# A mixture-of-experts layer whose weighted result rows are sent to their token's place during the products

## The chip, the cores and the metric

The kernel runs on one core of one Trainium2 chip. The metric is the time of one execution on the device, in microseconds (us). A core has a matrix engine (TensorE, PE), a vector engine (VectorE, DVE), a scalar engine (ScalarE, ACT), GpSimd (POOL) and SyncE (SP). SP, ACT and POOL issue DMA transfers, which run on 16 DMA engines. All arithmetic here is float32 unless a row says otherwise.

## What is computed

The program is a decoder of two layers on `x` (4 batches of 512 tokens of 256 numbers). Everything but its last step is the same in both kernels. The last step is a mixture of 8 experts, of which each token uses 2:

```
def _L1_ffn_ref(x, Wg, bg, W1, b1, W2, b2):
    gate_scores = softmax(x @ Wg + bg)
    topk_scores, topk_idx = top_k(gate_scores, 2)
    topk_scores = topk_scores / (sum(topk_scores) + 1e-08)
    for e in range(8):
        h = gelu(x @ W1[e] + b1[e])
        y = h @ W2[e] + b2[e]
        output = output + y * combine_w[..., e:e + 1]
    return output
x = x + _L1_ffn_ref(_layernorm(x), ...)
```

`combine_w` holds a token's two normalised scores at its two experts. W1[e] is 256x1024 and W2[e] 1024x256, 1 MB each.

## The kernel before, in words

All of this is in `mixture`, the last function that runs. Token tile t (t = 0 to 15, four to a batch) holds 128 tokens, one per partition. There are 5 stages, each a block of one program per engine, ended by a barrier of all engines (line 69).

- **mi** (L2428 to L2463). SP loads the 2 MB of `xs` in one DMA (L2431), then the gate's small weights, and waits for all. DVE fills `hid` with zeros (L2439); ACT writes them over the whole of `x_by_expert` in DRAM in three DMAs (L2453). POOL and DVE make small constants.
- **mn** (L2466 to L2511). DVE takes mean and variance of all 16 tiles (`norm_stats`, L97 and L100), POOL raises the variances to the power of minus one half (L107), DVE normalises tile by tile into `xn` (L2481). PE transposes (L2496), ACT copies each batch to `xTall` (L2511). When all is transposed PE forms the gate's scores (L2502), and DVE adds the bias in 16 instructions (L2485).
- **mg** (L2514 to L2618). DVE picks two experts per token, counts, and works out for each of the 4096 (token, expert) pairs its row in a list sorted by expert in which each expert begins at a multiple of 256 rows (`pos`, L2580). POOL then sends the rows of `xn` there with 32 indirect DMAs of 128 rows of 1 KB (L2618, 16 tiles times 2 experts). Meanwhile PE and DVE add the experts' second biases to `xs` (L2609, L2583).
- **ex** (L2622 to L2732). The sorted list has NTL = 23 tiles of 256 rows. For each tile SP loads the expert's W1 and W2 (L2631, L2632, three slots) and the rows `xg` (L2635, three slots), PE transposes them (L2664), DVE copies the transposes to `xgT` (L2722), PE multiplies by W1 (L2676), ACT applies bias and gelu (L2711), PE multiplies by W2 (L2688), DVE copies each half of the result to `yg` (L2732), and SP stores it to `y_by_expert` (L2639). PE's order is: transpose and first product of tile t+1, then second product of tile t.
- **mo** (L2736 to end). POOL gathers the result rows of each token tile with 32 indirect DMAs (L2746) into eight buffers `got`, DVE multiplies each by the pair's weight and adds it to `xs` (L2756, 32 times), SP stores each finished tile in 16 DMAs (L2764).

SP's order in ex is written by hand: `wait turned, rows(t), wait down, weights(t), results(t - 3)`. The y of tile t, half a, is ready when `down` reaches 2t + a + 1.

Of the kernel before, what the change touches and what calls it, by code (L numbers as in the profile page):

```python
# [22 lines left out]
P = 128  # L23
# [2363 lines left out]
def mixture(nc, es, dram, x5, out, psum, ident, nhalf, b1c):  # L2387
# [5 lines left out]
    WS, XS, GS = 3, 3, 8  # L2393
    x_sorted = nc.dram_tensor("x_by_expert", [NTL * TL, C], F32, kind="Internal").ap()
    y_sorted = nc.dram_tensor("y_by_expert", [NTL * TL, C], F32, kind="Internal").ap()
    xs, xn = sb("xs", [P, NT, C]), sb("xn", [P, NT, C])
# [3 lines left out]
    xg, xgT = sb("xg", [P, XS, TL // P, C]), sb("xgT", [P, 2, KT, TL])  # L2400
    yg = sb("yg", [P, 2, TL // P, C])
    got = sb("got", [P, GS, C])
# [17 lines left out]
    eps_var, rstd = sb("mev", [P, NT]), sb("mrstd", [P, NT])  # L2420

    w_in = [es.enter_context(nc.semaphore(f"expert_weights_in{i}")) for i in range(WS)]
    x_in = [es.enter_context(nc.semaphore(f"expert_rows_in{i}")) for i in range(XS)]
    y_out = [es.enter_context(nc.semaphore(f"expert_rows_out{i}")) for i in range(2)]
    cleared = es.enter_context(nc.semaphore("sorted_cleared"))
    sent = es.enter_context(nc.semaphore("rows_sorted"))

    with stage(nc, "mi", "in_", "zeroed") as (block, in_, zeroed):  # L2428
        @block.sync
        def _(sp):  # L2430
            sp.dma_start(xs[:, :, :].rearrange("p (b t) c -> p b t c", b=B), x5.rearrange("b p t c -> p b t c")).then_inc(in_, 16)  # L2431
# [3 lines left out]
            sp.wait_ge(in_, 16 * 4)  # L2435

        @block.vector
        def _(dve):
            dve.memset(hid[:, :, :, :], 0.0).then_inc(zeroed, 1)  # L2439
            dve.memset(before_me[:, :], 1.0).then_inc(zeroed, 1)  # L2440
            dve.memset(all_ones[:, :], 1.0)
            dve.memset(restart[:, :, 1:NT], 1.0)
            dve.memset(restart[:, :, 0:1], 0.0)

        @block.scalar
        def _(act):
            act.wait_ge(zeroed, 1)
            zeros = hid[:, :, :, :].rearrange("p s f n -> p (s f n)")
            rows = x_sorted.rearrange("(p r) c -> p (r c)", p=P)
            at = 0  # L2450
            while at < NTL * TL * C // P:
                n = min(2 * FT * TL, NTL * TL * C // P - at)
                act.dma_start(rows[:, at:at + n], zeros[:, 0:n]).then_inc(cleared, 16)  # L2453
                at += n

        @block.gpsimd
        def _(pool):
            pool.iota(idx[:, 0, :], [[1, NE]], base=0, channel_multiplier=0)
            pool.iota(count_u[:, :], [[1, 24]], base=0, channel_multiplier=0)
            pool.wait_ge(zeroed, 2)  # L2460
            pool.affine_select(before_me[:, :], before_me[:, :], [[1, P]], ALU.is_gt, 0.0, base=0,
                               channel_multiplier=-1)
    n_cleared = 16 * -(-(NTL * TL * C // P) // (2 * FT * TL))  # L2463


    with stage(nc, "mn", "dc", "var_ready", "rstd_ready", "normed", "turned", "copied", "gated", "logged") as (  # L2466
            block, dc, var_ready, rstd_ready, normed, turned, copied, gated, logged):
        on_vector, on_pool = norm_stats(nc, "mn", xs, stats, mv, rstd, eps_var, nhalf, NT, (dc, var_ready, rstd_ready))

        @block.gpsimd  # L2470
        def _(pool):
            on_pool(pool)

        @block.vector
        def _(dve):
            then = chained(dve, dc)
            dve.tensor_copy(iota[:, :], idx[:, 0, :])
            dve.tensor_copy(counted[:, :], count_u[:, :])
            on_vector(dve, then)
            for t in range(NT):  # L2480
                dve.tensor_scalar(xn[:, t, :], xs[:, t, :], mv[:, t, 0:1], rstd[:, t:t + 1],  # L2481
                                  ALU.subtract, ALU.mult).then_inc(normed, 1)
            for t in range(NT):
                dve.wait_ge(gated, t + 1)
                dve.tensor_tensor(lg[:, t, :], psum[:, 6, t * NE:(t + 1) * NE], bg[:, :], ALU.add)  # L2485

        @block.tensor
        def _(pe):
            for b in range(B):
                if b >= 2:  # L2490
                    pe.wait_ge(copied, b - 1)
                for t in range(QT):
                    tt = b * QT + t
                    pe.wait_ge(normed, tt + 1)
                    for k in range(KT):
                        last = pe.transpose(psum[:, 2 * (b % 2) + k, t * P:(t + 1) * P],  # L2496
                                            xn[:, tt, k * P:(k + 1) * P], ident[:, :])
                last.then_inc(turned, 1)
            for tt in range(NT):
                pe.wait_ge(copied, tt // QT + 1)  # L2500
                for k in range(KT):
                    last = pe.matmul(psum[:, 6, tt * NE:(tt + 1) * NE], xTall[:, k, tt * P:(tt + 1) * P], wg[:, k, :],  # L2502
                                     start=(tt == 0 and k == 0), stop=(k == KT - 1), skip_group_check=True)
                if tt == NT - 1:
                    last.then_inc(gated, NT)

        @block.scalar
        def _(act):
            for b in range(B):
                act.wait_ge(turned, b + 1)  # L2510
                act.copy(xTall[:, :, b * T:(b + 1) * T], psum[:, 2 * (b % 2):2 * (b % 2) + 2, :]).then_inc(copied, 1)  # L2511

# [275 lines left out]
```

## Time and profile of the kernel before

| what | us |
|---|---|
| median of 3 runs (lowest, highest) | 4335.82 (4323.85, 4353.62) |
| the profiled execution, its own time | 4334.44 |
| its span, first to last recorded event | 4332.6 |

So 1.84 us lie around the span. Of the span PE was busy 80%, DVE 51%, ACT 38%, POOL 21%. Times in the rows below count from the start of the span. A row of the timeline has start, duration, engine, line and operation; in square brackets stands how long the engine was idle before it and what released it.

### The profile page before, as it was taken

To read this page: it belongs to the slowest core of one execution; us is meant where nothing else is said; L and a number is where in the kernel's file an instruction comes from. 1 tells how busy PE (TensorE), PEld (TensorE's weight loads), DVE (VectorE), ACT (ScalarE), POOL (GpSimd) and SP (SyncE) were. 2 spreads that over 40 slices of the span, in tenths; PEclk is the share of its full clock that TensorE was granted. 3 is DMA by queue.
4 is the path that set the end of the run, shared out by engine and by line. 5 is a ranking of instruction groups with operands and counts; after the bars stand their busy time and mean duration, and the time that the engine had idled before them with its cause. 6 is when DMAs were issued, how large, how long until landed. Compare 5 with 4: busy or idle time off the path is not lost. (4 is left out here: it accounts for less than half of the span.)

```text
span 4332.6 us, 56718 instructions
## 1 busy us (share of the span) xinstructions
PE 3450.6 (80%) x21582; PEld 1893.0 (44%) x21582; DVE 2230.4 (51%) x4281; ACT 1642.5 (38%) x2455; POOL 905.5 (21%) x989
## 2 busy tenths in 40 slices
PE   3887678898887588898887788988875788946995
PEld 2423453426324345245334535264244543435884
DVE  3465766553464855734557764634648656430002
ACT  1343653342343733333345642423437433401221
POOL 0110542101201722011104512012006320120002
PEclk9889789999899799999898798999998899958997
DMA  4111102201202011111102012011120011034553
GB/s 80 37 55 59 16 7 74 62 19 36 67 12 73 1 42 61 41 35 42 55 20 54 1 42 83 19 40 42 50 73 1 30 66 48 30 115 155 173 175 119
DMA packets 244259, 239.67 MB, mean 55 GB/s; under 512 B 111902, under 2 KB 209420, under 8 KB 241548
## 3 DMA queue, kind: packets, MB, share of 16 engines
q1 hardware_dynamic: 234224, 217.91, 16.7%
q10 hardware_dynamic: 6684, 9.63, 0.7%
q0 software_dynamic: 3072, 8.39, 0.6%
q8 instruction: 177, 2.90, 0.3%
q14 instruction: 102, 0.84, 0.1%
HBM read 167.20 MB, written 68.68 MB: 54 GB/s over the span
## 5 line engine op out<-in xcount | busy, mean ns | idle before, releaser
L857 ACT ACTIVATE prob<-psum 128x1024 f32<-128x1024 f32 x384 | 372.2, 1021 | 559.1 <-PE psum L777 559.1
L1184 ACT ACTIVATE prob<-psum 128x1024 f32<-128x1024 f32 (+3 forms) x384 | 331.6, 914 | 443.7 <-PE psum L1104 443.7
L898 DVE TENSOR_REDUCE scr<-psum 128x1 f32<-128x512 f32 x576 | 371.4, 685 | 216.7 <-PE psum L764 212.9
L1222 DVE TENSOR_REDUCE stats<-psum 128x1 f32<-128x512 f32 (+3 forms) x576 | 334.3, 620 | 165.7 <-PE psum L1092 161.0
L1104 PE MATMUL psum<-stack 32*128 32x512 f32 (+3 forms) x1536 | 213.3, 626 | 63.2 <-ACT prob L1184 33.1
L774 PE MATMUL psum<-stack 32*128 32x512 f32 x1536 | 228.6, 665 | 33.2 <-DVE xo L888 24.7
L395 PE MATMUL psum<-ident 128*128 128x128 f32 x1736 | 220.2, 287 | 14.6 <-PEq L1809 9.6
L395 PEld LDWEIGHTS psum<-ident 128*128 128x128 f32 x1736 | 214.3, 203 | 24.7 <-issue 23.9
L805 PE MATMUL psum<-prob,ones_f 128*32 128x512 f32 x1536 | 206.8, 606 | 0.0
L1119 PE MATMUL psum<-prob,vbig 128*32 128x512 f32 (+3 forms) x1536 | 194.4, 580 | 4.3 <-ACT prob L1184 4.3
L2676 PE MATMUL psum<-xgT,ew 128*128 128x256 f32 x736 | 167.0, 386 | 18.0 <-DVE xgT L2722 18.0
L2732 DVE COPY yg<-psum 128x256 f32<-128x256 f32 x46 | 19.5, 425 | 308.5 <-PE psum L2688 308.5
L2711 ACT ACTIVATE hid<-psum,b1c 128x256 f32<-128x256 f32 x184 | 77.1, 470 | 257.6 <-PE psum L2676 257.6
L894 DVE TENSOR_REDUCE scr<-psum 128x4 f32<-128x2048 f32 x48 | 108.8, 2289 | 123.7 <-PE psum L757 123.6
L1218 DVE TENSOR_REDUCE stats<-psum 128x4 f32<-128x2048 f32 (+3 forms) x48 | 97.2, 2025 | 135.8 <-PE psum L1081 135.8
L579 POOL TENSOR_TENSOR x<-x,rows 128x256 f32<-128x256 f32 x32 | 22.1, 723 | 671.9 <-ACTq L64 581.6
L2688 PE MATMUL psum<-ew,hid 128*128 128x256 f32 x736 | 162.4, 379 | 0.0
L1610 POOL TENSOR_TENSOR xo<-xa,rows 128x256 f32<-128x256 f32 x32 | 22.2, 725 | 661.3 <-POOLq L1359 661.3
L2676 PEld LDWEIGHTS psum<-xgT,ew 128*128 128x128 f32 x736 | 139.4, 192 | 42.1 <-DVE xgT L2722 23.7
L1092 PE MATMUL psum<-w_mlp,stack 96*128 96x512 bf16 x384 | 134.6, 411 | 26.2 <-DVE stats L1222 16.2
L764 PE MATMUL psum<-w_mlp,stack 96*128 96x512 bf16 x384 | 126.6, 399 | 30.5 <-DVE scr L898 29.8
L2688 PEld LDWEIGHTS psum<-ew,hid 128*128 128x128 f32 x736 | 139.8, 190 | 19.0
(444 smaller groups left out, 6690.6 us busy)
## 6 DMA issues: line engine op xcount, KB each, us to landing
ew<-in_L_ffn_W SPq DMA_DIRECT2D x46, 1024.0 KB, 7.5
stack<-q_terms SPq DMA_DIRECT2D x144, 128.0 KB, 2.4
w_mlp<-in_L_xattn_a_li_w SPq DMA_DIRECT2D x16, 1024.0 KB, 7.3
q_terms<-parts SPq DMA_DIRECT2D x96, 128.0 KB, 2.1
stack<-k_terms SPq DMA_DIRECT2D x72, 128.0 KB, 2.7
w_mlp<-k_terms SPq DMA_DIRECT2D x36, 256.0 KB, 4.4
w_mlp<-a_terms SPq DMA_DIRECT2D x36, 256.0 KB, 4.9
a_keys<-stack SPq DMA_DIRECT2D x4, 2048.0 KB, 6.3
```

The costliest lines, as they stand in the source:

```text
L395: pe.matmul(psum[:, bank, at:at + P], ident[:, :], ident[:, :], start=True, stop=True, skip_group_check=True)
L774: pe.matmul(psum[:, j, :], KTg[W * j:W * j + W, g, kt * P:(kt + 1) * P], QTg[W * j:W * j + W, g, :], start=True, stop=False)
L805: last = pe.matmul(psum[W * j:W * j + W, 7, :], ones_f[:, :], prob[:, (2 * n + j // 2) % 4, j % 2, :], start=(kt == order[0]), stop=(kt == ...
L857: act.activation(prob[:, i % 4, :, :], psum[:, 2 * p:2 * p + 2, :], ACT.Exp, scale=scale).then_inc(exped, 1)
L898: dve.tensor_reduce(found[:, c:c + 1], ring(i), AX.X, ALU.max).then_inc(freed, 1)
L1092: pe.matmul(ring(i)[:, 0:n], MQ[0:ROWS, g % 2, j, t * P:(t + 1) * P], MK[0:ROWS, g % 2, j, h * BANK:h * BANK + n], start=not causal, stop= ...
L1104: last = pe.matmul(psum[:, j, q0:T], KTg[W * j:W * j + W, g, kt * P:(kt + 1) * P], QTg[W * j:W * j + W, g, q0:T], start=True, stop=True)
L1119: last = pe.matmul(psum[W * j:W * j + W, 6 + g % 2, q0:T], V[:, kt, g * P + W * j:g * P + W * j + W], prob[:, (2 * n + j // 2) % 4, j % 2, ...
L1184: act.activation(prob[:, i % 4, :, q0:T], psum[:, 2 * p:2 * p + 2, q0:T], ACT.Exp, scale=scale).then_inc(exped, 1)
L1222: dve.tensor_reduce(found[:, c:c + 1], ring(i)[:, 0:keys_of(t)], AX.X, ALU.max).then_inc(freed, 1)
L2676: last = pe.matmul(psum[:, m % 4, (f % 2) * TL:(f % 2 + 1) * TL], w1[:, t % WS, k, f * P:(f + 1) * P], xgT[:, t % 2, k, :], start=(f % 2 = ...
L2688: last = pe.matmul(psum[:, 4 + a, 0:C], hid[:, t % 2, f, a * P:(a + 1) * P], w2[:, t % WS, f, :], start=(f == 0), stop=(f == FT - 1))
```

## The change

1. Each sorted row becomes 258 numbers long: 256 values, the pair's weight (column 256), and as an integer the row of a new DRAM tensor `y_by_row` to which its result belongs (column 257). `xn` exists twice, once for each of the token's two experts, because weight and place differ. ACT makes the second copy. Place numbers are written by POOL (iota), weights by DVE in mg.
2. The whole of `x_by_expert` is preset, not with zeros alone: blank rows have value and weight 0 and a place of their own behind the real ones. `blank` (23 rows of 258 numbers per partition) is made by POOL in the memory of `ew1` and written by ACT in two DMAs, with new place numbers between them.
3. mi and mn are one stage. `xs` is loaded in four DMAs, one per batch; statistics, power, normalising, transposing and gate go batch by batch. The bias is one instruction.
4. In ex, DVE's copy of y becomes a multiplication by the row's weight. POOL sends each half tile (128 rows of 1 KB) with an indirect DMA to its places in `y_by_row`, 46 in all; SP no longer stores results. `xg` has 4 slots.
5. mo is gone. At the end of ex, when all result rows have landed, SP loads the first experts' plane and ACT the second's, in 4 DMAs each (512 KB); DVE adds both to `xs` per batch and SP stores a batch with one DMA.

The diff, cut to its core:

```diff
+    WS, XS = 3, 4
+    ROW, HALF = C + 2, NTL * TL // P // 2
+    x_sorted = nc.dram_tensor("x_by_expert", [NTL * TL, ROW], F32, kind="Internal").ap()
+    y_rows = nc.dram_tensor("y_by_row", [2 * NT * P + NTL * TL, C], F32, kind="Internal").ap()
...
         @block.sync
         def _(sp):
+            for b in range(B):
+                sp.dma_start(xs[:, b * QT:(b + 1) * QT, :], x5[b]).then_inc(batch_in[b], 16)
...
+            sp.wait_ge(in_, 16 * 3)
...
         @block.gpsimd
         def _(pool):
+            pool.memset(blank[:, :, 0:C + 1], 0.0)
+            number_blanks(pool, 0)
+            pool.iota(idx[:, 0, :], [[1, NE]], base=0, channel_multiplier=0)
+            pool.iota(count_u[:, :], [[1, 24]], base=0, channel_multiplier=0).then_inc(counts_in, 1)
+            for b in range(B):
+                pool.wait_ge(var_ready, b + 1)
+                tiles = slice(b * QT, (b + 1) * QT)
+                pool.tensor_tensor(rstd[:, tiles], eps_var[:, tiles], nhalf[:, tiles], ALU.pow).then_inc(rstd_ready, 1)
+            pool.wait_ge(cleared, 16)
+            number_blanks(pool, 1)
+            pool.wait_ge(ones_in, 1)
+            pool.affine_select(before_me[:, :], before_me[:, :], [[1, P]], ALU.is_gt, 0.0, base=0,
+                               channel_multiplier=-1)
+            for i in range(2):
+                pool.iota(xn[i][:, :, C + 1].bitcast(U32), [[1, NT]], base=i * NT * P, channel_multiplier=NT)
...
+            measure(0)
+            for b in range(B):
+                if b + 1 < B:
+                    measure(b + 1)
+                normalise(b)
...
+            turn(0)
+            pe.wait_ge(in_, 16 * 3)
+            for b in range(B):
+                if b + 1 < B:
+                    turn(b + 1)
+                pe.wait_ge(copied, b + 1)
...
+            clear_half(0)
             for b in range(B):
                 act.wait_ge(turned, b + 1)
                 act.copy(xTall[:, :, b * T:(b + 1) * T], psum[:, 2 * (b % 2):2 * (b % 2) + 2, :]).then_inc(copied, 1)
+                act.copy(xn[1][:, b * QT:(b + 1) * QT, 0:C], xn[0][:, b * QT:(b + 1) * QT, 0:C])
+            clear_half(1)
...
             for i in range(2):
+                dve.tensor_tensor(xn[i][:, :, C], top[:, :, i], mxr, ALU.mult)
...
-                        ap=pos[:, i, t:t + 1], axis=0), in_=xn[:, t, :], in_offset=None).then_inc(sent, 16)
+                        ap=pos[:, i, t:t + 1], axis=0), in_=xn[i][:, t, :], in_offset=None).then_inc(sent, 16)
...
-            for t in range(XS, NTL):
-                sp.wait_ge(turned, t - XS + 1)
-                rows(t)
+            for t in range(WS, NTL):
                 sp.wait_ge(down, halves * (t - WS + 1))
                 weights(t)
-                results(t - WS)
-            for t in range(NTL - WS, NTL):
-                results(t)
+                if t >= XS:
+                    sp.wait_ge(turned, t - XS + 1)
+                    sp.wait_ge(y_out[t % 2], 16 * halves * ((t - XS) // 2 + 1))
+                    rows(t)
+            wait_for_results(sp)
+            fetch_results(sp, 0)
+            ov = out.rearrange("b (t p) c -> b p t c", p=P)
+            for b in range(B):
+                sp.wait_ge(added, 2 * (b + 1))
+                sp.dma_start(ov[b], xs[:, b * QT:(b + 1) * QT, :]).then_inc(stored, 16)
...
+        @block.gpsimd
+        def _(pool):
+            for t in range(NTL):
+                for a in range(halves):
+                    pool.wait_ge(yready, halves * t + a + 1)
+                    pool.indirect_dma_start(out=y_rows[:, :], out_offset=bass.IndirectOffsetOnAxis(
+                        ap=xg[:, t % XS, a, C + 1:C + 2].bitcast(U32), axis=0), in_=yg[:, t % 2, a, :],
+                        in_offset=None).then_inc(y_out[t % 2], 16)
...
+            wait_for_results(act)
+            fetch_results(act, 1)
...
-                        dve.wait_ge(y_out[t % 2], 16 * (t // 2))
-                    dve.tensor_copy(yg[:, t % 2, a, :], psum[:, 4 + a, 0:C]).then_inc(yready, 1)
+                        dve.wait_ge(y_out[t % 2], 16 * halves * (t // 2))
+                    dve.tensor_scalar(yg[:, t % 2, a, :], psum[:, 4 + a, 0:C], xg[:, t % XS, a, C:C + 1], None,
+                                      ALU.mult).then_inc(yready, 1)
+            for b in range(B):
+                dve.wait_ge(both_back[b], 32)
+                mine = xs[:, b * QT:(b + 1) * QT, :]
+                for i in range(2):
+                    dve.tensor_tensor(mine, mine, back[i][:, b * QT:(b + 1) * QT, :], ALU.add).then_inc(added, 1)
+                    dve.wait_ge(added, 2 * b + i + 1)
```

## Rows read from the trace of the kernel before

**Rows 1.** Busy time by stretch: the scatters of mg; ex; mo.

```profile
core 0: us, PE busy (x) PEld busy (x) DVE busy (x) ACT busy (x) POOL busy (x), PEclk, DMA share, GB/s
3862.30:3902.70 40.40, 12.81 (x28) 7.11 (x28) 6.28 (x16) 0.00 (x0) 30.95 (x32) 0.50 0.29 101
...
3930.30:4285.40 355.10, 336.59 (x1564) 290.93 (x1564) 35.44 (x69) 78.42 (x185) 0.00 (x0) 0.99 0.44 150
4285.40:4332.60 47.20, 0.00 (x0) 0.00 (x0) 15.50 (x32) 0.00 (x0) 30.32 (x32) 0.53 0.48 139
```

**Rows 2.** The chain that ended last, in order of time: start, duration, what.

```profile
4248.65 7.17 PE psum L2676 x32
...
4263.20 0.70 DVE xgT L2722
...
4271.12 13.83 PE psum L2688 x64
4285.43 2.00 DMA y_by_expert<-yg
```

**Rows 3.** Timeline of mi and mn.

```profile
3805.24 0.40 SPq L2431 DMA_DIRECT2D xs<-x_after_layers  x1
...
3815.12 5.32 DVE L97 BATCH_NORM_STATS2 mstats<-xs 128x6 f32<-128x256 f32 x16
...
3824.89 5.26 DVE L2481 TENSOR_SCALAR xn<-xs,mmv,mrstd 128x256 f32<-128x256 f32 x16 [3.04 <-POOL mrstd L107]
3825.36 6.21 PE L2496 MATMUL psum<-ident,xn 128*128 128x128 f32 x32 [25.48 <-DVE xn L2481]
3827.36 1.01 ACT L2511 COPY xTall<-psum 128x1024 f32<-128x1024 f32 x1 [34.74 <-PE psum L2496]
...
3831.41 11.36 PE L2502 MATMUL psum<-wg,xTall 128*128 128x8 f32 x64
3842.80 1.26 DVE L2485 TENSOR_TENSOR lg<-psum,bg 128x8 f32<-128x8 f32 x16 [12.65 <-PE psum L2502]
```

**Rows 4.** Busy time by stretch while `xs` is loaded; columns as in rows 1.

```profile
3805.00:3808.00 3.00, 0.00 (x0) 0.00 (x0) 1.83 (x1) 0.00 (x0) 0.24 (x2) 0.50 0.52 117
3808.00:3811.00 3.00, 0.00 (x0) 0.00 (x0) 2.07 (x5) 0.00 (x0) 0.29 (x1) 0.50 1.02 404
```

**Rows 5.** POOL's groups by shape: busy us, mean ns, idle before.

```profile
L107 POOL TENSOR_TENSOR rstd<-eps_var,nhalf 128x4 f32<-128x4 f32 x12 | 12.2, 1016 | 206.1 <-DVE eps_var L102 206.1
...
L2122 POOL MEMSET vbig<- 128x1024 f32 x4 | 3.8, 952 | 0.0
```

**Rows 6.** DMA issues of the last 533 us: the clearing's last transfer.

```profile
x_by_expert<-hid ACTq DMA_DIRECT2D x1, 1792.0 KB, 17.6
```

**Rows 7.** Timeline of mg: the places, the first scatter.

```profile
3861.80 0.18 DVE L2580 CAST pos<-pos_f 128x32 uint32<-128x32 f32 x1
...
3862.28 1.23 POOL L2618 DMA_INDIRECT x_by_expert<-xn,pos  x1 [37.43 <-DVE pos L2580]
```

**Rows 8.** SP issues the rows of a tile of ex; landing times of `xg`.

```profile
4035.51 0.52 SPq L2635 DMA_DIRECT2D xg<-x_by_expert  x1
...
DMA to landing us min/median/max: 2.5/7.9/12.0
```

**Rows 9.** DVE's groups by shape.

```profile
L2732 DVE COPY yg<-psum 128x256 f32<-128x256 f32 x46 | 19.5, 425 | 308.5 <-PE psum L2688 308.5
L2237 DVE TENSOR_SCALAR vbig<-psum 128x512 f32<-128x512 f32 x8 | 5.5, 686 | 9.6 <-PE psum L2180 9.6
L342 DVE TENSOR_TENSOR vbig<-xh,ob 128x1024 f32<-128x1024 f32 x4 | 4.9, 1225 | 0.1
```

**Rows 10.** Timeline of mo: first gather, first addition, last addition.

```profile
4287.69 0.99 POOL L2746 DMA_INDIRECT got<-y_by_expert,pos  x1 [384.96 <-DMA y_by_expert<-yg]
...
4290.50 0.48 DVE L2756 SCALAR_TENSOR_TENSOR xs<-got,col,xs 128x256 f32<-128x256 f32 x1 [5.11 <-DMA got<-y_by_expert,pos]
...
4329.50 0.49 DVE L2756 SCALAR_TENSOR_TENSOR xs<-got,col,xs 128x256 f32<-128x256 f32 x1 [0.90 <-DMA got<-y_by_expert,pos]
```

More of the change, by code:

```diff
@@ L2392, in mixture @@
     NT = B * QT
[L2393 to L2396, printed above, removed]
+    WS, XS = 3, 4
+    ROW, HALF = C + 2, NTL * TL // P // 2
+    x_sorted = nc.dram_tensor("x_by_expert", [NTL * TL, ROW], F32, kind="Internal").ap()
+    y_rows = nc.dram_tensor("y_by_row", [2 * NT * P + NTL * TL, C], F32, kind="Internal").ap()
+    xs, xn = sb("xs", [P, NT, C]), [sb(f"xn{i}", [P, NT, ROW]) for i in range(2)]
     xTall = sb("xTall", [P, KT, NT * P])
@@ L2437, in _, with measure @@
         @block.vector
         def _(dve):
-            dve.memset(hid[:, :, :, :], 0.0).then_inc(zeroed, 1)
-            dve.memset(before_me[:, :], 1.0).then_inc(zeroed, 1)
+            then = chained(dve, dc)
+            def measure(b):
+                dve.wait_ge(batch_in[b], 16)
+                for t in range(b * QT, (b + 1) * QT):
+                    last = dve.bn_stats(stats[:, t, :], xs[:, t, :])
+                then(last)
+                for t in range(b * QT, (b + 1) * QT):
+                    last = dve.bn_aggr(mv[:, t, :], stats[:, t, :])
+                then(last)
+                tiles = slice(b * QT, (b + 1) * QT)
+                dve.tensor_scalar(eps_var[:, tiles], mv[:, tiles, 1], EPS, None, ALU.add).then_inc(var_ready, 1)
@@ L2441, in _, with normalise @@
+            def normalise(b):
+                dve.wait_ge(rstd_ready, b + 1)
+                for t in range(b * QT, (b + 1) * QT):
+                    dve.tensor_scalar(xn[0][:, t, 0:C], xs[:, t, :], mv[:, t, 0:1], rstd[:, t:t + 1],
+                                      ALU.subtract, ALU.mult).then_inc(normed, 1)
+            dve.memset(before_me[:, :], 1.0).then_inc(ones_in, 1)
             dve.memset(all_ones[:, :], 1.0)
@@ L2443, in _ @@
             dve.memset(restart[:, :, 0:1], 0.0)
+            measure(0)
[3 more added lines that the diff above has]
+                normalise(b)
+            dve.wait_ge(counts_in, 1)
+            dve.tensor_copy(iota[:, :], idx[:, 0, :])
+            dve.tensor_copy(counted[:, :], count_u[:, :])
+            dve.wait_ge(in_, 16 * 3)
+            dve.wait_ge(gated, 1)
+            dve.tensor_tensor(lg[:, :, :], psum[:, 6, 0:NT * NE].rearrange("p (t e) -> p t e", e=NE),
+                              bg[:, :].unsqueeze(1).to_broadcast([P, NT, NE]), ALU.add)
@@ new lines, in _, with turn @@
+        @block.tensor
+        def _(pe):
+            def turn(b):
+                if b >= 2:
+                    pe.wait_ge(copied, b - 1)
+                pe.wait_ge(normed, QT * (b + 1))
+                for t in range(QT):
+                    for k in range(KT):
+                        last = pe.transpose(psum[:, 2 * (b % 2) + k, t * P:(t + 1) * P],
+                                            xn[0][:, b * QT + t, k * P:(k + 1) * P], ident[:, :])
+                last.then_inc(turned, 1)
+            turn(0)
[4 more added lines that the diff above has]
+                pe.wait_ge(copied, b + 1)
+                for tt in range(b * QT, (b + 1) * QT):
+                    for k in range(KT):
+                        last = pe.matmul(psum[:, 6, tt * NE:(tt + 1) * NE], xTall[:, k, tt * P:(tt + 1) * P], wg[:, k, :],
+                                         start=(tt == 0 and k == 0), stop=(k == KT - 1), skip_group_check=True)
+            last.then_inc(gated, 1)
@@ L2463, in mixture @@
[L2463 to L2508, printed above, removed]
@@ L2509, in _, with clear_half @@
+            sorted_rows = x_sorted.rearrange("(p i r) c -> p i (r c)", p=P, i=2)
+            def clear_half(i):
+                act.wait_ge(blank_in, i + 1)
+                act.dma_start(sorted_rows[:, i, :], blank.rearrange("p r n -> p (r n)")).then_inc(cleared, 16)
+            clear_half(0)
             for b in range(B):
@@ L2618, in _, with fetch_results, wait_for_results @@
                     pool.indirect_dma_start(out=x_sorted[:, :], out_offset=bass.IndirectOffsetOnAxis(
-                        ap=pos[:, i, t:t + 1], axis=0), in_=xn[:, t, :], in_offset=None).then_inc(sent, 16)
-    with stage(nc, "ex", "turned", "turned_in", "up", "acted", "down", "yready") as (
-            block, turned, turned_in, up, acted, down, yready):
+                        ap=pos[:, i, t:t + 1], axis=0), in_=xn[i][:, t, :], in_offset=None).then_inc(sent, 16)
+    with stage(nc, "ex", "turned", "turned_in", "up", "acted", "down", "yready", "added", "stored") as (
+            block, turned, turned_in, up, acted, down, yready, added, stored):
         halves = TL // P
+        def fetch_results(eng, i):
+            plane = y_rows[i * NT * P:(i + 1) * NT * P, :].rearrange("(p t) c -> p t c", t=NT)
+            for b in range(B):
+                tiles = slice(b * QT, (b + 1) * QT)
+                eng.dma_start(back[i][:, tiles, :], plane[:, tiles, :]).then_inc(both_back[b], 16)
+        def wait_for_results(eng):
+            for i in range(2):
+                eng.wait_ge(y_out[i], 16 * halves * ((NTL + 1 - i) // 2))
         @block.sync
```

71 lines of the change are left out of this document (19 added, 52 removed).

## The prediction

> **What bounds the kernel now.** The change touches only what runs after about 3800 us of the span, so I read the stretches there first, then the chain of waits inside them, then the timeline at both ends. The busy time by stretch [rows 1] shows three things. In ex, 355.1 us for 23 tiles, PE is busy 336.6 us and the DMA engines 44%: PE sets the pace, 15.4 us a tile. In the 40.4 us of mg's scatters only POOL is near full (32 in 30.95 us busy), DMA at 29%. In mo, 47.2 us, PE is idle, POOL is busy 30.3 us and DVE 15.5 us. The chain in order of time [rows 2] says the same of ex: first product 7.17 us, second product (13.83 us for two), and between them only DVE's copy to `xgT`, 0.70 us. No DMA stands in it until the last result is stored (2.00 us). At the head [rows 3] each engine works alone for a while: 2 MB are loaded, DVE takes all statistics, POOL all powers (DVE idle 3.04 us), and PE begins at 3825.36, 20 us after the load was issued at 3805.24. From there to the last gate product PE works without a gap, 6.21 + 11.36 = 17.6 us. So the change can gain at the head (what lies before PE's start) and in mo, and has to add nothing in ex.
>
> **Head: mi and mn become one batched stage.** Loading. Up to 3808.00 0.35 MB moved, after that 404 GB/s [rows 4]; so data flowed from about 3807.1, 1.9 us after the issue. A batch of 0.52 MB needs 1.3 us more: batch 0 is there at 3808.4, the others 1.3 us apart. DVE. From the first statistics to the normalising it spent 3824.89 - 3815.12 - 3.04 = 6.7 us on 16 tiles [rows 3], 1.7 a batch; with two more chained waits I take 2.0. Batch 0 is measured at 3810.4. POOL first zeroes `blank`, 23 x 257 = 5911 numbers; a MEMSET of 1024 took 0.952 us [rows 5], which makes 5.5 us, and three iotas 0.4 (two took 0.24 us [rows 4]): free at 3811.2. A power of 4 columns took 1.02 us [rows 5]: 3812.2. DVE measures batch 1 meanwhile (to 3812.4), then normalises batch 0, 4 x 0.33 = 1.3 us [rows 3]: PE starts at 3813.8 and not 3825.4. It transposes batch 0 (1.55 us) and then waits 1.7 us, for DVE has to measure batch 2 and normalise batch 1 (3817.1). After that DVE is ahead (3.3 us a batch against 1.55 + 2.84 of PE) and ACT too: its copy took 1.01 us [rows 3] and the added copy to the second `xn` I take at as much, 2.0 us a batch. PE ends at 3813.8 + 17.6 + 1.7 = 3833.1. The 16 bias additions (1.26 us) become one, some 0.3: 3833.5 against 3844.06. **Head: -10.5 us.** Ends of this term: -8 where PE also waits for ACT or the small weights, whose DMAs now queue behind `xs`; -12 where the wait of 1.7 us is hidden.
>
> Clearing costs nothing. Its second half can go only after the first has landed and POOL has renumbered. The first is issued at 3811, and the last and slowest of the three before landed 17.6 us after its issue beside the load of `xs` [rows 6]: at the latest 3829, before ACT's last copy is done at 3831. The second then lands by 3849 at worst, and POOL asks for it some 18 us after the head's end, when the places are ready, at 3851. POOL's waits in this stage hold up only iotas and the mask, which are due in mg. If the first half came 5 us later still, the head would end that much later.
>
> **mg.** Two more small DVE products before the counting: a CAST of 128x32 took 0.18 us [rows 7], so +0.3 us (0.2 to 0.4). The scatters keep their number; 32 in 40.4 us, 1.26 each, by POOL [rows 1]. Their rows are 1032 B and not 1024 B. No row has such a length. If POOL's work goes by descriptors, nothing changes; if every row became two pieces, it would be 0.96 more each, +31 us. I take 0, as the work seen is per index and DMA stands at 29%; +31 is a rival. `sent` and the start of ex stay: six weight loads, then rows.
>
> **ex.** Removed from SP: 23 stores. Moved: `rows(t)` goes behind `weights(t)` and gets a wait for the scatter of tile t-4. Queued behind that wait on SP are the next weights only; and tile t-4's scatter was issued a whole tile (15.4 us) before, while a gather was over 2.8 us after its start [rows 10], so it never holds. Within a pass the rows are issued in the same place as before, behind two weight loads (at 4035.51 in one pass [rows 8], some 2 us into it) and land after 7.9 us in the median. But PE wanted them two tiles later, and now one: they are there after about 9.8 of 15.4 us, 5.6 us spare. Bytes do not change (256 KB of results either way). DVE: the copy to `yg` took 0.425 us and becomes a multiplication from PSUM; a TENSOR_SCALAR of 512 from PSUM took 0.686 [rows 9], the same as the copy of 512 to `xgT`, 0.70 [rows 2], so 0 (bounds 0 to +0.06, the latter the 0.48 us of the three-operand form [rows 10]; it stands just before the `xgT` copy, thus 22 x 0.06 = +1.3 us). POOL works beside it: 46 times about 1.3 us in 355 us of idle. It delays nobody unless `yg` is wanted again, two tiles later. **ex: 0 us.**
>
> **Tail.** From the last `yg` (4285.4) it was 47.2 us [rows 1]. Now, in the old clock: POOL starts 0.3 us later (3861.98 to 3862.28 [rows 7]), 4285.7; a gather was usable 4290.50 - 4287.69 = 2.8 us after its start [rows 10], a scatter I take alike (ends 2.0, the plain store's time [rows 2], and 4): 4288.5. SP and ACT issue eight loads; first data 1.9 us later, 4290.4. Batch b needs 1.05 MB, 2.6 us at 404 GB/s [rows 4]; from the second on a store of 0.52 MB, 1.3 us, mixes in. Loads of batch 3 are there at 4290.4 + 4 x 2.6 + 2 x 1.3 = 4303.4. Its two additions of 128x1024 took 1.23 each [rows 9]: 4305.9. Before, from the end of the last addition (4329.99 [rows 10]) to the end of the span it was 2.6 us with a store of 128 KB; 512 KB need 0.9 more: 4309.4. So 24.0 us for 47.2. **Tail: -23.2 us**; with the ends of scatter and load (stores all hidden: 4306; all four mixed in and the scatter at 4: 4313) -27 to -19.
>
> At this place a rule can be weighed. Rows 4 have the DMA engines moving 404 GB/s from DRAM. The Trainium skill, "DMA: Bandwidth & Descriptors", Specifications, gives a limit of about 358 GB/s from HBM for a core; by it the 4.2 MB of loads and 1.0 MB of stores ahead of the last batch would take 14.5 us instead of 13.0, and the sum be 1.5 us higher. The trace does not agree, and the sum goes by the row.
>
> **Sum.** -10.5 + 0.3 + 0 - 23.2 = -33.4 us. The profiled execution took 4334.44 us, of which 1.84 around the span stay: 4301.0. Its time is 1.4 us below the median of 4335.82, within the runs' spread. 1% of this kernel, about what a measurement can tell from no change, is 43 us: the forecast lies under it.
>
> **Rivals.**
> - *Rows come late in ex (slower).* Mechanism: the scatters of 1 KB rows share the DMA engines with 2 MB of weights a tile, and the rows stand last in SP's queue with one tile of lead. For: they now come after the weights, and the lead halves. Against: DMA is at 44%, bytes are equal, 5.6 us are spare. It decides from a landing of 13.5 us on; each us beyond costs 19 us (tiles 4 to 22). At 7.9 x 2 = 15.8 us it is 2.3 x 19 = 44 us: 4345.
> - *Long rows double POOL's scatter.* For: no row of this length in the trace. Against: above. 4301 + 31 = 4332.
> - *The head is not gained* (clearing or zeroing slower than taken, so that POOL gives the first power late). If `blank` cost 1.9 ns a number, twice the row's, everything slides 5.5 us: 4306.5.
> - *The tail is shorter and the head too*: PE never waits after its start, loads of SP and ACT overlap the landing: -12 and -27, 4296.
> - *The change does not do what it says*: the first `rows` wait or the shared memory of `blank` and `ew1` would order things anew. All of it lies before the first weights, so no time comes from it.
>
> **How the numbers follow.** Forecast, 4301 with its own terms: 0.66. Late rows 0.04, long rows 0.06, head not gained 0.12, shorter at both ends 0.12. The bounds of the terms alone give 4295 to 4309, and the runs shown lie 12 below and 18 us above their median, so the range is 4283 to 4324; late rows and most of long rows are left out. Faster by over 1% needs 43 us: the last case with a lucky spread, 0.12. Slower by over 1% needs late rows at more than double: 0.02. Within 1%: 0.86.
>
> **What would show it.** PE's first transpose of the layer 11.6 us nearer to the load's issue than now; mg's scatters still 1.26 us apart; 23 tiles in 355 us with no wait of PE for `xg`; `yg` at 0.42 us; 24 us from the last `yg` to the end, with loads at 400 GB/s and additions of 1.2 us. Wrong would be scatters at 1.5 us and more, a DMA on PE's chain in ex, or powers late behind the MEMSET.

## The result, and where the time went

The kernel with the change took 4286.35 us (median of 4 runs, 4278.36 to 4292.19), the kernel before beside it 4338.8 us; the ratio is 0.9893 with the interval 0.987 to 0.9915. A later comparison, in the experiments below, gave 4305.12 against 4326.89 us, 0.9943 (0.992 to 0.9967). The forecast was 4301 us with a range of 4283 to 4324. So the first median lies 3 us inside the lower end of the range, and the first ratio is just past the 1% that the prediction had given a chance of 0.12; the second is not.

The profiled execution of the changed kernel took 4278.36 us, its span is 4276.6 us: 56.0 less than before, while the forecast was 33.4. So first the question which part of the 56.0 us belongs to the change. The last addition of the decoder (L1672, the same code in both kernels) starts at 3799.9 us before and at 3778.6 after: 21.3 us were gained in code that nobody touched. From that addition to the end it is 532.7 us before and 498.0 after: **34.7 us** in the changed part. All that follows is measured from that addition, piece by piece; a piece ends where the next begins.

| piece | before | after | difference | forecast |
|---|---|---|---|---|
| decoder's last addition to PE's first transpose | 25.5 | 13.8 | -11.7 | -11.6 |
| to the end of the gate's scores | 18.7 | 22.3 | +3.6 | +1.1 |
| to the places (`pos`) | 17.9 | 16.2 | -1.7 | +0.3 |
| 32 scatters of rows | 40.4 | 40.5 | +0.1 | 0 |
| last scatter to PE's first transpose of rows | 27.6 | 26.4 | -1.2 | 0 |
| products, to the last `yg` | 355.1 | 355.4 | +0.3 | 0 |
| last `yg` to the end | 47.2 | 23.1 | -24.1 | -23.2 |
| **in all** (with 0.3 between places and scatters, both) | 532.7 | 498.0 | -34.7 | -33.4 |

The busy time by stretch, after. The rows are the new head, the scatters, what lies between them and PE, the products and the tail; [rows 1] has three of these before.

```profile
core 0: us, PE busy (x) PEld busy (x) DVE busy (x) ACT busy (x) POOL busy (x), PEclk, DMA share, GB/s
3781.50:3814.70 33.20, 20.57 (x96) 20.10 (x96) 13.69 (x59) 7.83 (x8) 10.82 (x12) 0.51 0.58 236
...
3831.10:3871.60 40.50, 12.82 (x28) 7.12 (x28) 6.36 (x16) 0.00 (x0) 30.99 (x32) 0.50 0.28 101
3871.60:3898.00 26.40, 0.00 (x0) 0.00 (x0) 0.00 (x0) 0.00 (x0) 0.07 (x1) 0.50 0.78 265
3898.00:4253.50 355.50, 336.93 (x1564) 291.12 (x1564) 37.11 (x69) 78.54 (x185) 43.29 (x45) 0.99 0.44 151
4253.50:4276.60 23.10, 0.00 (x0) 0.00 (x0) 9.80 (x9) 0.00 (x0) 0.96 (x1) 0.56 0.78 278
```

In the products PE is as busy as before (336.9 us) although POOL now works 43.3 us beside it, at the same DMA share of 0.44. In the tail the DMA share went from 0.48 to 0.78 and POOL has one transfer left of 32.

The timeline of the head, after; [rows 3] before.

```profile
3783.78 5.03 POOL L2453 MEMSET ew<- 128x5911 f32 x1 [24.32 <-POOLq L69]
...
3787.07 1.40 DVE L2476 BATCH_NORM_STATS2 mstats<-xs 128x6 f32<-128x256 f32 x4 [2.73 <-DMA xs<-x_after_layers]
...
3789.20 1.03 POOL L2460 TENSOR_TENSOR mrstd<-mev,nhalf 128x4 f32<-128x4 f32 x1
...
3790.92 1.38 DVE L2487 TENSOR_SCALAR xn<-xs,mmv,mrstd 128x256 f32<-128x256 f32 x4
...
3792.36 1.97 PE L2515 MATMUL psum<-ident,xn 128*128 128x128 f32 x8 [13.83 <-DVE xn L2487]
...
3797.40 3.42 PE L2527 MATMUL psum<-wg,xTall 128*128 128x8 f32 x16
...
3807.43 6.83 PE L2527 MATMUL psum<-wg,xTall 128*128 128x8 f32 x32
...
3814.38 0.29 DVE L2504 TENSOR_TENSOR lg<-psum,bg 128x128 f32<-128x128 f32 x1 [14.02 <-PE psum L2527]
```

DVE takes its first statistics 3.3 us after the load is issued, where it was 9.9 us; POOL's 5.03 us of zeroing end just when the first variances are there; PE starts at 3792.4. But its passes are longer: 16 gate passes in 3.42 us and 32 in 6.83 are 0.21 us each, where [rows 3] have 64 in 11.36, 0.18 each. The granted clock tells why: stretches from PE's unbroken work, first in the changed kernel, then in the kernel before, columns as above.

```profile
3796.00:3799.00 3.00, 3.00 (x17) 3.00 (x15) 2.86 (x13) 1.67 (x3) 1.25 (x1) 0.50 0.57 245
3799.00:3802.00 3.00, 3.00 (x16) 3.00 (x17) 1.35 (x6) 0.60 (x1) 0.74 (x4) 0.50 0.02 5
3802.00:3805.00 3.00, 3.00 (x16) 3.00 (x16) 0.00 (x0) 1.96 (x2) 0.00 (x0) 0.50 0.00 0
```

```profile
3826.00:3829.00 3.00, 3.00 (x16) 3.00 (x15) 3.00 (x10) 1.01 (x1) 0.00 (x0) 0.50 0.15 62
3829.00:3832.00 3.00, 3.00 (x24) 3.00 (x22) 1.15 (x4) 2.28 (x3) 0.00 (x0) 0.75 0.00 0
3832.00:3836.00 4.00, 4.00 (x29) 4.00 (x29) 0.00 (x0) 0.66 (x1) 0.00 (x0) 0.74 0.00 0
...
3829.00:3830.00 1.00, 1.00 (x7) 1.00 (x6) 1.00 (x4) 0.93 (x1) 0.00 (x0) 0.50 0.00 0
3831.00:3832.00 1.00, 1.00 (x13) 1.00 (x11) 0.00 (x0) 1.00 (x2) 0.00 (x0) 1.00 0.00 0
3833.00:3834.00 1.00, 1.00 (x11) 1.00 (x10) 0.00 (x0) 0.00 (x0) 0.00 (x0) 0.97 0.00 0
3834.00:3835.00 1.00, 1.00 (x7) 1.00 (x6) 0.00 (x0) 0.00 (x0) 0.00 (x0) 0.50 0.00 0
```

After, PE is busy all the time at 0.50 (1.2 GHz) and does 16 passes in 3 us. Before, the clock stood at 1.00 (2.4 GHz) for about 3.5 us, from 3830.5 to 3834.0, and PE did 11 to 13 passes in 1 us there, for 6 or 7 outside. The 0.75 and 0.74 of the longer stretches are means over both levels.

The products: `yg` and the landing of the rows, [rows 9] and [rows 8] before.

```profile
L2789 DVE TENSOR_SCALAR yg<-psum,xg x46: 483/484/484, 3921.4 to 4253.0; 128x256 f32<-128x256 f32 x46
...
DMA to landing us min/median/max: 2.4/5.9/11.5
```

The tail, after ([rows 10] before):

```profile
4253.02 0.48 DVE L2789 TENSOR_SCALAR yg<-psum,xg 128x256 f32<-128x256 f32 x1 [2.97 <-PE psum L2743]
4253.78 0.96 POOL L2707 DMA_INDIRECT y_by_row<-yg,xg  x1 [2.49 <-DVE yg L2789]
4256.18 2.19 SPq L2665 DMA_DIRECT2D xTall<-y_by_row  x4
4256.18 2.39 ACTq L2665 DMA_DIRECT2D ew<-y_by_row  x4
4261.45 1.23 DVE L2795 TENSOR_TENSOR xs<-xs,xTall 128x1024 f32<-128x1024 f32 x1 [7.95 <-DMA ew<-y_by_row]
...
4269.95 1.22 DVE L2795 TENSOR_TENSOR xs<-xs,xTall 128x1024 f32<-128x1024 f32 x1 [0.57 <-DMA ew<-y_by_row]
4271.21 1.23 DVE L2795 TENSOR_TENSOR xs<-xs,ew 128x1024 f32<-128x1024 f32 x1
```

The scatter is done 2.4 us after its start, the first pair of planes is there 5.3 us after the loads are issued, the last 13.8 us after; two additions and a store follow, 6.7 us to the end.

### The profile page after: what moved, and what is told of

It reads as the page before. It is cut to its first block and busy times, and to the rows that moved or that the text cites. A ratio compares the mean times of both kernels' runs of the same rounds, so it can differ in the third digit from the quotient of the medians.

```text
span 4276.6 us, 56648 instructions
## 1 busy us (share of the span) xinstructions
PE 3428.9 (80%) x21582; PEld 1882.1 (44%) x21582; DVE 2225.2 (52%) x4246; ACT 1647.2 (39%) x2459; POOL 928.3 (22%) x1011
## 5 line engine op out<-in xcount | busy, mean ns | idle before, releaser
L774 PE MATMUL psum<-stack 32*128 32x512 f32 x1536 | 227.2, 661 | 32.2 <-DVE xo L888 24.7
L2789 DVE TENSOR_SCALAR yg<-psum,xg 128x256 f32<-128x256 f32 x46 | 22.2, 484 | 307.1 <-PE psum L2743 307.1
L1092 PE MATMUL psum<-w_mlp,stack 96*128 96x512 bf16 x384 | 134.1, 410 | 26.4 <-DVE stats L1222 16.4
```

Of the source, the lines that this page charges most:

```text
L774: pe.matmul(psum[:, j, :], KTg[W * j:W * j + W, g, kt * P:(kt + 1) * P], QTg[W * j:W * j + W, g, :], start=True, stop=False)
L1092: pe.matmul(ring(i)[:, 0:n], MQ[0:ROWS, g % 2, j, t * P:(t + 1) * P], MK[0:ROWS, g % 2, j, h * BANK:h * BANK + n], start=not causal, stop= ...
```

## Experiments

**Is the decoder's gain part of the change?** Both kernels again, unchanged, beside each other.

> The kernel before, unchanged, as a control. Two executions of the kernels differed by 56 us of span, of which 21.3 us lie ahead of the changed code (the last addition of the decoder starts at 3799.9 us before, at 3778.6 after). Chance theory (granted clock differs from run to run in equal code): the ratio to the kernel before is 1.000 within 0.3%, and the start of that last addition in this run falls anywhere in 3775 to 3805. Rival (the changed program makes the decoder faster): it falls at 3795 to 3805 here.

> The changed kernel again. Chance theory: ratio 0.992 (35 us of 4336), the last decoder addition anywhere in 3775 to 3805. Rival: ratio 0.987, that addition at 3775 to 3783 again. Both: from that addition's start to the end 498 us.

Measured: for the kernel before against itself the ratio is 0.9995 (0.9976 to 1.0015); the changed kernel 0.9943 (0.992 to 0.9967). The decoder's last addition starts at 3788.3 and at 3791.5 us. This study has fourteen profiles, all with the same decoder: in the two of the kernel before it starts at 3799.9 and 3788.3 us, in the twelve of the changed kernel and its variants anywhere between 3778.6 and 3810.1 us. The rival falls: the decoder's time goes up and down by itself, a little further even than the 3775 to 3805 that I had given, and the mean is 3794.1 for the two and 3796.7 for the twelve. The granted clock goes with it: over the whole span it was 0.905 in the profile with the earliest mark and 0.896 and 0.895 in the two with the latest. One place where it differs is this window of the decoder, before and after:

```profile
100.00:130.00 30.00, 26.75 (x129) 20.92 (x127) 8.28 (x27) 3.52 (x4) 1.01 (x1) 0.66 0.00 1
```

```profile
100.00:130.00 30.00, 25.87 (x149) 17.88 (x149) 8.90 (x26) 7.64 (x10) 2.69 (x3) 1.00 0.00 1
```

The granted clock was 0.66 in the one and 1.00 in the other, and PE did 129 and 149 instructions. What makes the throttle grant less in one execution than in another isn't shown. The changed part on the other hand repeats to 0.6 us: 532.7 and 532.1 before, 498.0 and 498.4 after. So 34 us, 0.992 of the kernel, is the effect; the first comparison overstates it (its upper end, 0.9915, just misses it) and the second holds it at the lower end of its interval.

**The tail alone.** Results stored in sorted order, 32 gathers and weighting at the end, on the changed kernel:

```diff
-                        ap=xg[:, t % XS, a, C + 1:C + 2].bitcast(U32), axis=0), in_=yg[:, t % 2, a, :],
+                sp.dma_start(y_sorted[t * TL:(t + 1) * TL, :].rearrange("(p a) c -> p a c", a=halves),
+                             yg[:, t % 2, :, :]).then_inc(y_out[t % 2], 16)
...
+                pool.indirect_dma_start(out=got[:, n % 8, :], out_offset=None, in_=y_sorted[:, :],
+                                        in_offset=bass.IndirectOffsetOnAxis(ap=pos[:, i, t:t + 1], axis=0)).then_inc(
+                                            gathered[n % 8], 16)
```

> The changed kernel with results stored in sorted order and gathered and weighted by 32 indirect transfers at the end, as before. If the tail is worth what the trace says (24.1 us of 34.7), the stretch from the decoder's last addition to the end is 498 + 24 = 522 us and the last result to the end 47 us. Rival (the scatters in the product stage cost something there): the product stage, first transpose to last result, falls from 355.5 to 354.5 or less and the stretch is 521 or less.

Measured: 522.5 us from the decoder's last addition to the end, tail 47.3 us, products 355.8 us (355.4 and 355.9 in the two profiles of the changed kernel); ratio 0.9982 (0.9965 to 1.0). The tail is worth 24.2 us, and the scatters beside PE, with DVE's multiplication in place of the copy, cost nothing that can be seen. The tail's stretch:

```profile
4265.90:4313.30 47.40, 0.00 (x0) 0.00 (x0) 15.62 (x33) 0.00 (x0) 30.27 (x32) 0.54 0.49 139
```

**The head alone.** Loading and norms in two stages and unbatched, rows and blanks as in the changed kernel:

```diff
-            for b in range(B):
-                sp.dma_start(xs[:, b * QT:(b + 1) * QT, :], x5[b]).then_inc(batch_in[b], 16)
+            sp.dma_start(xs[:, :, :].rearrange("p (b t) c -> p b t c", b=B), x5.rearrange("b p t c -> p b t c")).then_inc(in_, 16)
...
+    with stage(nc, "mn", "renumbered", "dc", "var_ready", "rstd_ready", "normed", "turned", "copied", "gated", "logged") as (
...
+            on_vector(dve, then)
```

> The changed kernel with loading and norms in two stages, unbatched, as before (long rows, blanks and second copy stay; only the batching and the merging go). If the head's worth is the batching, the stretch from the decoder's last addition to the end is 498 + 8 to 10 = 506 to 508 us. Rival (the 1.7 us gained between the gate and the places, and 1.2 us after the scatters, come with the new tail's code and not with the head): it is 506 with these two gains still there; if they come with the head they are gone too, 509.

Measured: 506.0 us, so the head is worth 8.0 us. To PE's start 24.9 us, then 17.2 us to the scores, 17.4 to the places, 27.5 behind the scatters, tail 23.2. It is not the head of before to the last detail: from PE's start to the scores that took 18.7 us. The clock rose here by 3833.0, 3.1 us behind PE's start and after some 15 of its transposes, and 5.1 us behind it before.

```profile
3829.88:3833.00 3.12, 3.12 (x15) 3.09 (x16) 3.12 (x11) 1.11 (x2) 0.00 (x0) 0.52 0.00 0
3833.00:3834.00 1.00, 1.00 (x11) 0.93 (x9) 1.00 (x5) 1.00 (x2) 0.00 (x0) 1.00 0.00 0
```

So the tail's 24.2 and the head's 8.0 us make 32.2 of the 34; 1.5 us of what is missing is this. Most of the two unforeseen gains goes with the head (1.2 of 1.7 us to the places, 1.1 us behind the scatters), and one cause is in sight:

```profile
3849.48 0.31 ACT L2599 ACTIVATE ex<-lg 128x128 f32<-128x128 f32 x1
3851.07 0.28 DVE L2534 TENSOR_REDUCE col<-ex 128x16 f32<-128x128 f32 x1 [2.23 <-issue]
```

DVE is idle for 2.23 us. The profile calls it issue, but until 3849.79, for 0.95 us, DVE needs ACT's `ex` (the changed kernel waits 0.99 us for it at this place); the other 1.28 us are a wait for nothing that the profile shows. The kernel before has such a pause of 2.56 us, at its line 2522, 2.39 in its second profile, and the changed kernel none in that piece. It moves with the code, not with the data. What it is wasn't tried. Fetching of instructions is one guess, and the traces fit it without proving it: a DMA queue of the kind "instruction" moved one packet of some 8 KB between 3846.0 and 3846.5 in the pause of the kernel before (3845.47 to 3848.03), between 3834.5 and 3835.0 in its second profile (pause to 3836.31), and between 3849.0 and 3849.5 here, each time 1.3 to 2.1 us before DVE went on. In the changed kernel one moved between 3817.0 and 3817.5 and DVE made no pause beyond its wait for ACT.

**Why PE's clock stayed at 0.50 in the new head.** Two orders of PE's work:

```diff
-            turn(0)
-            pe.wait_ge(in_, 16 * 3)
             for b in range(B):
-                if b + 1 < B:
-                    turn(b + 1)
+                turn(b)
+            pe.wait_ge(in_, 16 * 3)
+            for b in range(B):
                 pe.wait_ge(copied, b + 1)
```

> The changed kernel with the gate products of all batches behind all transposes, as before the change; batching of loads, statistics and transposes stays. From PE's first transpose to the gate's scores it was 18.7 us before and 22.3 us after, at a granted clock of 0.50 throughout after, while before it rose to 0.90 and 0.67 for six microseconds behind 32 transposes without a gap. Theory (what raises the clock is transposes without gaps): here they still come 8 per 3.3 us, so the clock stays at 0.50, all 64 gate passes run at 0.2 us, and the piece becomes 12 + 13.7 = 25.5 us. Rival (the few-column gate products in between keep the clock low): it rises as before and the piece is 12 + 11.4 = 23.4 us or less.

Measured: clock 0.50 throughout, transposes still in groups of 8 (the last two groups on end), 24.0 us from the first transpose to the scores (PE's start was 1.5 us later, 15.3; the end thus 39.3 us behind the decoder's last addition, 36.1 in the changed kernel). The rival's clock is wrong. My 25.5 us was 1.5 too long, which is also what PE started later: the end came where I had put it. The second has in addition `pe.wait_ge(normed, NT)` ahead of the first transpose:

> The changed kernel, but PE waits until all 16 tiles are normalised, then does the 32 transposes without waits and the gate products last: a late start bought for transposes without gaps. Theory (transposes without gaps are what raised the clock before the change): the granted clock rises above 0.50 a few us behind PE's start, and from first transpose to scores it takes 17.5 to 18.7 us as before, with the start at 21.5 to 22 us behind the decoder's last addition. Rival (something else of the new stage, its transfers or ACT's second copy, keeps the clock at 0.50): 19.5 us and more.

Measured: PE starts at 21.8 us, and from there it is 17.8 us to the scores. Its stretches of 3 us from PE's start on:

```profile
3831.10:3834.10 3.00, 2.22 (x11) 2.22 (x12) 0.98 (x5) 0.21 (x1) 0.79 (x4) 0.50 0.00 0
3834.10:3837.10 3.00, 3.00 (x16) 3.00 (x15) 0.00 (x0) 3.00 (x4) 0.00 (x0) 0.50 0.00 0
3837.10:3840.10 3.00, 3.00 (x26) 3.00 (x24) 0.00 (x0) 3.00 (x4) 0.00 (x0) 0.88 0.30 127
3840.10:3843.10 3.00, 3.00 (x21) 3.00 (x20) 0.00 (x0) 1.32 (x2) 0.00 (x0) 0.69 1.19 506
3843.10:3846.10 3.00, 3.00 (x16) 3.00 (x16) 0.00 (x0) 0.00 (x0) 0.00 (x0) 0.50 0.89 380
```

The clock rises as before the change, beside ACT's second copies, so these don't hold it down. It falls again although PE goes on without a gap, with the gate's 128x8 products. So in this kernel it rose while transposes ran without a gap, after some 15 (head undone), 22 and 24 (the kernel before, twice) and 27 of them (here). It did not in any of the ten profiles whose head has groups of 8. That is a difference in what PE did, not yet the throttle's rule: with the gates last the final 16 transposes came without a gap too, at 0.50. In the head undone it rose while DVE was still normalising, so that doesn't hold it down either. What the throttle goes by stays open; starting early is still worth more, 36.1 us against 39.6.

**Do the scatters disturb the products?** Every half tile is sent twice:

```diff
+                    for y_to in (y_more, y_rows):
+                        pool.indirect_dma_start(out=y_to[:, :], out_offset=bass.IndirectOffsetOnAxis(
```

> The changed kernel with every half tile of results sent twice, the second time to a tensor that nobody reads. It doubles POOL's 46 transfers and adds 256 KB a tile to the DMA engines. Theory (PE sets the pace, rows have spare time): the product stage stays 355.4 to 356.5 us and only the tail grows by POOL's second transfer, 1.3 us. Rival of the prediction (scatters make rows late): rows land after more than 13.5 us, PE waits for them, and the stage is 370 us or more.

Measured: products 355.9 us, rows land after 5.8 us in the median, tail 24.4 us (+1.3). With twice the scatters PE waits no longer than with one. The slower rival of the prediction falls. The other side of the same question, less lead for the rows:

```diff
-    WS, XS = 3, 4
+    WS, XS = 3, 3
...
-                    sp.wait_ge(y_out[t % 2], 16 * halves * ((t - XS) // 2 + 1))
+                    sp.wait_ge(y_out[(t - XS) % 2], 16 * halves * ((t - XS) // 2 + 1))
```

> The changed kernel with three slots for the rows in place of four, so that the rows of tile t wait for the scatter of tile t-3, whose second half begins when SP asks for it. Theory (5 us and more of spare time before PE wants them): rows are issued about 2.5 us later and PE does not wait; product stage 355.4 to 356.0 us. Rival (the fourth slot is needed): each tile waits, 1 us or more each, stage 375 us or more.

Measured: products 355.1 us, the whole stretch 499.2 us (PE's first transpose was 1.2 us late, a variation of the head that has nothing to do with it). What SP waited for in the products: engine, line, releaser, us in total, times, longest.

```profile
SPq L2674 <- PE psum L2743: 185.9, 20, 32.7
SPq L2692 <- DMA y_by_row<-yg,xg: 103.8, 20, 6.1
```

SP now waits 5.2 us a tile for the scatter, twice what I had expected; that the second half's scatter shares the DMA engines with the weights just issued is the likely reason, not a tested one. But the rows then land after 3.1 us in the median and not 5.9. In one tile they were issued 6.0 us behind the first weights and not 1.0, so by these medians they come about 2 us later than with four slots, still in time. The fourth slot is not needed.

**One queue for the final loads.**

```diff
+            for b in range(B):
+                for i in range(2):
+                    fetch_one(sp, i, b)
...
-            wait_for_results(act)
-            fetch_results(act, 1)
```

> The changed kernel with all eight final loads issued by SP, in the order in which they are needed, and none by ACT. Theory (the 16 DMA engines are full either way, 367 to 420 GB/s, and only the issue counts): the tail, last result to end, stays 23.1 us, or becomes up to 1 us longer, for SP's issue of 0.4 to 0.5 us each and because its stores queue behind. Rival (two queues move more than one): the first addition starts later than 8 us after the last result and the tail is 26 us or more.

Measured: tail 23.8 us against 23.1 (22.9 to 23.3 in the seven profiles with the changed tail as it is); the first addition starts 7.8 us after the last result, as in the changed kernel (8.0), the last pair of planes comes 14.5 us after the first issue and not 13.8. Both queues feed the same engines. The Trainium skill, "DMA: Bandwidth & Descriptors", Issuing engines are not separate DMA queues, says that, and this run agrees: 0.7 us is all that the second queue saves, by a single profile.

**Two ideas that follow.** Of the changed kernel's 498 us the piece behind the scatters, 26.4 us, has no engine computing: the stage's barrier, SP's issues (with a pause of 5.78 us among them, last section) and the loads. `sched` is known before the scatters begin, and the DMA engines are at 0.28 while they run:

```diff
+            sp.wait_ge(cleared, n_cleared)
+            sp.wait_ge(scheduled, 1)
+            for t in range(WS):
+                load_weights(sp, t)
...
-            for t in range(WS):
-                weights(t)
             sp.wait_ge(sent, 16 * 2 * NT)
```

> The changed kernel with the weights of the first three tiles loaded in the stage before, as soon as the schedule is known and the blanks are written, beside POOL's scatters (DMA share there 0.28). Theory (26.4 us from the last scatter to PE's first transpose is mostly 6 MB of weights ahead of the rows in the DMA engines, 11.5 us, and 10 us of SP's issue): this piece shrinks to 10 to 13 us, and the stretch from the decoder's last addition to the end to 482 to 485 us. Rival (the loads slow POOL's scatters or are fetched code's wait in truth): scatters at over 1.27 us each, or the piece stays above 20 us.

Measured: scatters 40.5 us as before, though the DMA share beside them was 1.00 from 3855 to 3870, then 6.6 us to PE's first transpose in place of 26.4; the stretch is 478.5 us, 19.5 less than the changed kernel and better than expected.

```profile
3893.53 0.96 POOL L2666 DMA_INDIRECT x_by_expert<-xn,pos  x1 [0.30 <-issue]
3894.80 0.96 POOL L2666 DMA_INDIRECT x_by_expert<-xn,pos  x1 [0.30 <-issue]
3899.59 1.77 SPq L2693 DMA_DIRECT2D xg<-x_by_expert  x4
3902.41 0.72 PEld L2730 LDWEIGHTS psum<-ident,xg 128*128 128x128 f32 x4 [34.85 <-DMA xg<-x_by_expert]
```

The rows land 2.8 us after their issue when no weights are ahead of them. The second idea is a finer tail, 8 pieces for 4:

```diff
-            for b in range(B):
-                tiles = slice(b * QT, (b + 1) * QT)
+            for b in range(CH):
+                tiles = slice(b * PT, (b + 1) * PT)
```

> The changed kernel with the final loads, additions and stores in 8 pieces of two token tiles in place of 4 of four. Theory (behind the last load stand two additions of 1.23 us and a store of 512 KB; halves of both go): the tail becomes 23.1 - 1.2 - 0.6 = 21.3 us. Rival (16 loads cost SP and ACT 0.4 to 0.5 us each and rows of 2 KB move slower): 23 us or more.

Measured: tail 22.4 us, 0.7 less in place of 1.8 (the whole stretch 498.6 us: behind the scatters it took 28.1 us in this program, 1.7 more). Additions of 128x512 took 0.69 us (two make more than one of 1.23), and DVE, which had pauses before, now runs all sixteen without one and ends last:

```profile
4279.80 0.69 DVE L2797 TENSOR_TENSOR xs<-xs,xTall 128x512 f32<-128x512 f32 x1
4280.53 0.69 DVE L2797 TENSOR_TENSOR xs<-xs,ew 128x512 f32<-128x512 f32 x1
4281.26 0.69 DVE L2797 TENSOR_TENSOR xs<-xs,xTall 128x512 f32<-128x512 f32 x1
4281.98 0.69 DVE L2797 TENSOR_TENSOR xs<-xs,ew 128x512 f32<-128x512 f32 x1
```

Both together:

> Both that promise something: weights of the first three tiles loaded beside the scatters (the run before: stretch 478.5 us against 498) and the tail in 8 pieces. If the gains add, the stretch from the decoder's last addition to the end is 476.5 to 478.5 us against 532.4 of the kernel before, 54 to 56 us or 1.27% of 4330: ratio to the kernel before 0.987, within the interval's 0.2%. If they don't, the tail is 24 us or the first transposes wait again.

Measured: 478.4 us, ratio 0.9873 (0.9854 to 0.9893), median 4278.41 us against 4328.77. The early weights are the whole of it; the finer tail's 1 us (22.3) was taken by a start of PE 1.5 us later (15.3 us) in this program.

## Why the prediction came out as it did

The time lay in the range and went the way forecast. The working forecast 33.4 us, the changed part gave 34.7 and 33.7 us in the two pairs of profiles; the first medians are 52 us apart because more than that differed: the profiled pair has 21.3 us ahead of the mark, in the decoder, beside a different granted clock; no step of the prediction could have told that. There is luck in how near the sum came: the head's passes cost 2.6 us more than forecast, and the places (2.0 us sooner than forecast), the piece behind the scatters (1.2) and the tail (0.9) gave more than that back. The first two were not foreseen.

- **The tail** was read right and sized 1 us too dear: -24.1 for -23.2. Scatter to landing took 2.4 us (2.8 taken from the gather), the last planes came 16.5 us after the last `yg` (18.0), two additions 2.5; from their end to the end of the span it was 4.2 us, where 3.5 had been calculated. The limit of about 358 GB/s weighed there would have made it longer; the DMA engines moved 367 to 420 GB/s in five of the six stretches of 2 us between 4258 and 4270. The Trainium skill, "DMA: Bandwidth & Descriptors", Specifications, gets that figure by dividing a stack's 716 GB/s between two cores. One core runs here, and the trace shows that it isn't held to the half: the prediction had read the row as a limit for any core.
- **PE's start** came 11.7 us sooner, 11.6 forecast. The terms hold one by one: first batch there at 3787.1, 3.3 us after the issue (3.2), statistics 2.0 us a batch, `blank` 5.03 us (5.5), power 1.03.
- **From PE's start to the scores** is the step that failed: "PE ends at 3813.8 + 17.6 + 1.7". The 1.7 us of wait were 1.3, but 17.6 was a sum of durations of which about 3.5 us had been worked at a clock of 1.00, reached during 32 transposes without a gap. Batched, PE stayed at 0.50, was busy for 20.6 us and the piece took 22.3 us for some 19.7 forecast: +2.6. The bounds of this term (-12 to -8) held what came, -8.1, but named other causes for their ends.
- **mg**, up to the places, was to cost +0.3 and gave 1.7: the two added products are there (0.19 us each), but a pause of 2.56 us in DVE's issue, which I had left in the sum as if it were work, is gone.
- **The scatters' price does not depend on the row's 1032 B**: 1.27 us apart, 0.96 busy. That rival falls.
- **The products**: +0.3 us, which is less than the 0.5 between two profiles of one kernel. The multiplication took 0.484 us, the upper bound that I had given, not the 0.425 that I took; by the sum it could cost 1.3 us, and no cost is seen: with the plain copy and no scatters (tail undone) the stage took 355.8 us. In a tile of the changed kernel it ran from 4001.31 to 4001.79, beside PE's transposes, which ended at 4001.71. Rows were there in time, and the runs with double scatters and with three slots show how far from its threshold the slower rival was.
- **Clearing** was hidden as worked out; the first half landed 10 us after its issue.

## What to carry to other kernels

Measure a change from a mark that both programs share: here the untouched decoder moved by 31 us from profile to profile, and the changed part of one program by 0.6. When work on TensorE is cut into batches to start it sooner, take its passes at the lower clock level and see whether the sooner start still pays. And where weights are loaded right before they are needed, ask when their address is known: 19.5 us, nearly as much as the tail gave, lay beside the scatters, and nobody had them on the list.

## What was not expected of the hardware

- TensorE's granted clock stayed at 0.50 (1.2 GHz) for 18 us of unbroken work in the new head, 8 transposes in turn with 16 gate products, behind a first group of 8 and a wait of 1.3 us. It rose to 1.00 (2.4 GHz) in the four profiles in which 24 or 32 transposes came without a gap, and was back at 0.50 while the gate products of 8 columns ran on without one.
- Pauses in DVE's issue, 2.56 and 2.39 us in the kernel before, 1.28 with the head undone, stand at another instruction in each program, or at none, with the same work around them.
- SP pauses alike. The chain in order of time, changed kernel, between the weights of the first and the second tile:

```profile
3876.92 0.39 SPq L2677
3877.31 5.78 issue
3883.09 0.28 SPq L2674
```

It waits 5.78 us for nothing that the profile's chain shows; an "instruction" packet moved between 3881 and 3882, as in DVE's pauses. With the weights loaded early such a pause (first weights at 3853.75, second at 3860.07) costs nothing.
